# TensorE's rounds of all three stages, and attention's rounds on four engines, written out instead of looped

## The reference

```python
# tokens: normalised correlation with a 31 x 31 template, mean over 3 channels
result = conv(image, norm_template)           # same for the mean and the mean square
std    = sqrt(m2 - m1 * m1)
h      = mean_over_channels(result / (std + 1e-9)); nan -> 0      # 16 x 256 x 256

# attention: 16 query heads, 8 key heads, width 64, causal
q, k = l2norm(heads(rmsnorm(h) @ Wq)), l2norm(heads(rmsnorm(h) @ Wk));  v = ...
attn = softmax(causal(tanh(q k / 50) * 50 / 8))
h    = layernorm(h + (attn @ v) @ Wout)

# MLP, 256 -> 1024 -> 1024 -> 1024 -> 256
m = silu(x @ w1 * s1) * (x @ w2 * s2)
m = gelu(m @ h1 * t1);  m = gelu(m @ h2 * t2)
out = layernorm(h + m @ w3 * s3)
```

## Time and profile before

| | before |
|---|---|
| median of 3 runs | 1764.07 us (1761.74 to 1764.49) |
| the profiled execution | 1769.29 us |
| its span, first to last instruction | 1767.4 us |
| instructions in it | 33166 |
| TensorE busy | 1717.2 us, 97% of the span |
| VectorE busy | 1150.9 us, 65% |
| ScalarE busy | 911.1 us, 52% |
| GpSimd busy | 418.1 us, 24% |
| mean granted clock of TensorE | 0.99 of full speed |

### The profile page before, as it was taken

The page is one execution under the profiler, slowest core; times in us unless marked ns, Lnnn a source line. Parts: engine busy times, 40 slices in busy tenths (PEclk is TensorE's granted clock), DMA queues, the critical chain, the costliest instruction groups (busy, mean ns, idle before and its releaser), DMA issues. The chain is left out here.

```text
span 1767.4 us, 33166 instructions
## 1 busy us (share of the span) xinstructions
PE 1717.2 (97%) x12280; PEld 1512.0 (86%) x12280; DVE 1150.9 (65%) x2223; ACT 911.1 (52%) x1309; POOL 418.1 (24%) x517
## 2 busy tenths in 40 slices
PE   6999999999999999999999998999999999999998
PEld 5999998999987888888888887888888888888886
DVE  6999898898996878888878874342414141514242
ACT  7756555566657877886887873222222221222221
POOL 2000000000012222222222221434434333434343
PEclk9999999999999999999999998999999999999999
DMA  6222312214103002102001113500000000000000
GB/s 198 104 98 95 130 56 112 87 63 160 49 1 109 18 27 82 34 18 90 26 26 52 31 34 131 191 25 1 25 1 24 0 25 1 24 0 25 1 13 13
DMA packets 35923, 97.19 MB, mean 55 GB/s; under 512 B 3114, under 2 KB 23722, under 8 KB 31539
## 3 DMA queue, kind: packets, MB, share of 16 engines
q1 hardware_dynamic: 35762, 94.96, 15.8%
HBM read 82.33 MB, written 24.15 MB: 60 GB/s over the span
## 5 line engine op out<-in xcount | busy, mean ns | idle before, releaser
L671 PE MATMUL conv<-w,x 128*128 128x368 f16 (+5 forms) x3960 | 455.4, 279 | 1.9 <-issue 1.9
L671 PEld LDWEIGHTS conv<-w,x 128*128 128x128 f16 x3960 | 428.8, 146 | 27.1 <-issue 2.7
L1480 ACT ACTIVATE raw_c<-ring,sh 128x512 f32<-128x512 f32 x128 | 87.5, 689 | 334.4 <-PE ring L1583 334.3
L1492 DVE CAST ha_hi<-raw_c 128x512 fp32r<-128x512 f32 x128 | 83.8, 655 | 200.5 <-ACT raw_c L1480 198.3
L1439 POOL TENSOR_TENSOR ha_lo<-raw_c,ha_hi 128x512 fp32r<-128x512 f32 x128 | 165.3, 1291 | 190.9 <-DVE ha_hi L1492 190.9
L912 POOL TENSOR_SCALAR_AFFINE_SELECT probs<-probs 128x256 f32<-128x256 f32 x256 | 117.5, 482 | 362.0 <-ACT probs L981 362.0
L1583 PE MATMUL ring<-hb_lo,wh 128*128 128x512 f32 x512 | 199.5, 390 | 0.0
L1583 PE MATMUL ring<-ha_lo,wh 128*128 128x512 f32 x512 | 199.5, 390 | 0.0
L1583 PE MATMUL ring<-ha_hi,wh 128*128 128x512 f32 x512 | 199.4, 390 | 0.0
L1583 PE MATMUL ring<-hb_hi,wh 128*128 128x512 f32 x512 | 199.4, 389 | 0.0
L1179 PE MATMUL mixed<-v,probs 128*128 128x65 f32 x1536 | 188.5, 273 | 0.2 <-POOL probs L912 0.2
(11 more groups left out here) (168 smaller groups left out, 3290.2 us busy)
## 6 DMA issues: line engine op xcount, KB each, us to landing
xt<-x_columns_in SPq DMA_DIRECT2D x12, 1163.0 KB, 5.2
xp<-x_patches_in SPq DMA_DIRECT2D x12, 1152.0 KB, 5.2
hidden_words<-hidden_weights_in SPq DMA_DIRECT2D x8, 1408.0 KB, 9.1
words<-hidden_words SPq DMA_DIRECT2D x32, 352.0 KB, 3.0
wh<-hidden_words SPq DMA_DIRECT2D x8, 1024.0 KB, 10.6
tokens<-planes SPq DMA_DIRECT2D x4, 1024.0 KB, 5.6
h<-tokens SPq DMA_DIRECT2D x4, 1024.0 KB, 5.6
attended<-h SPq DMA_DIRECT2D x8, 512.0 KB, 3.4
```

The lines of the kernel that those rows point to most:

```text
L671: ins = pe.matmul(out, xs[:, c, RI - 1 - i:RI - 1 - i + NR, :, x].rearrange("p r g -> p (r g)"), w, start=(t == 0), stop=(t == size - 1), ...
L1480: act.activation(raw[:, u % 4], bank, ACT.Gelu, scale=scale[:, m:m + 1]).then_inc(s_gelu, 1)
L1492: dve.tensor_copy(dst[0][:, u % KH], raw[:, u % 4]).then_inc(s_hi, 1)
```

## The change

`planes` and `every_lot` get an argument `unrolled`, which only TensorE sets; `every_part` loses its loop for every engine that uses it. The rounds are then written one behind the other into the program by the Python that builds it, with the round number as a constant. What each round does, and in which order, stays as it is.

```diff
-        def planes(eng, body, first, start=0):
+        def planes(eng, body, first, start=0, unrolled=False):
 
 
             first()
-            with eng.Fori(start, GROUPS - 1) as g:
-                for c in range(CHANNELS):
-                    body(g, c, g * CHANNELS + c, False)
+            if unrolled:
+                for g in range(start, GROUPS - 1):
+                    for c in range(CHANNELS):
+                        body(g, c, g * CHANNELS + c, False)
+            else:
+                with eng.Fori(start, GROUPS - 1) as g:
+                    for c in range(CHANNELS):
+                        body(g, c, g * CHANNELS + c, False)
             for c in range(CHANNELS):
                 body(GROUPS - 1, c, LAST - CHANNELS + 1 + c, True)
...
-            planes(pe, body, first, 1)
+            planes(pe, body, first, 1, unrolled=True)
...
 def every_part(emit, eng):
 
-    with eng.Fori(0, GROUPS - 1) as g:
+    for g in range(GROUPS - 1):
         emit(BODY, g)
     emit(FINAL, GROUPS - 1)
...
-        def every_lot(eng, lot):
-
-            with eng.Fori(0, GROUPS - 1) as g:
-                for parity in range(2):
-                    lot(g, parity, False)
+        def every_lot(eng, lot, unrolled=False):
+
+            if unrolled:
+                for g in range(GROUPS - 1):
+                    for parity in range(2):
+                        lot(g, parity, False)
+            else:
+                with eng.Fori(0, GROUPS - 1) as g:
+                    for parity in range(2):
+                        lot(g, parity, False)
             for parity in range(2):
                 lot(GROUPS - 1, parity, parity == 1)
...
             def lots(exact):
-                every_lot(pe, lambda g, parity, last: lot(g, parity, last, exact))
+                every_lot(pe, lambda g, parity, last: lot(g, parity, last, exact), unrolled=True)
```

## The result

| | before | after |
|---|---|---|
| median | 1764.28 us, 6 runs (1761.74 to 1771.77) | 1753.11 us, 6 runs (1752.22 to 1754.22) |
| profiled execution, its span | 1769.29, 1767.4 us | 1753.59, 1751.8 us |
| mean granted clock in it | 0.990 | 0.993 |

The medians differ by 11.2 us, a ratio of 0.9937. The measured ratio with its 95% interval is 0.9924 (0.9907 to 0.9942), which is 13.4 us (10.2 to 16.4); the interval holds the 11.2 as well. The two traces differ by 15.6 us of span. Why the medians lie closer together than the traces is what experiment 1 is about.

The account below looks back on a forecast made before the run. TensorE, busy 97% of the span, was taken as the bound, so only its idle or lower-clock time counted. Seam savings of 3.75, 4.95 and 5.76 us, 14.5 in all, off 1764.07 gave 1749.6 us, range 1746.0 to 1756.5.

Parts of the forecast that it names:

- The gaps are taken branches that wait for code: At TensorE's seams between looped rounds: five idle gaps, 9.2 us, come from five taken branches waiting for code.
- The sum by seams: Saving at taken-branch seams, priced against loop exits: token stage 3.75, attention 4.95, MLP 5.76, sum 14.5 us.
- Register waits at zero: Waits on constants instead of registers gain zero; rival: 4.4 us on TensorE's path, 1745.2 us, chance 0.08.
- The other engines at zero: ScalarE, VectorE, GpSimd and SyncE, looped or written out, count zero; ScalarE's code comes 2.4 us late in attention.
- The length of the lead: TensorE's sequencer runs 1.9 us ahead of the array, hiding that much branch; queue depth would suggest 3.7 us.
- From the trace to the median: The 14.5 us priced in the 1769.29 us profiled execution, taken off the 1764.07 us median, gives 1749.6 us.
- The case called "less": Unprofiled runs lack the 5 us clock part or have cheaper branches: only 9.5 us saved, 1754.6 us, chance 0.18.
- The slower case: Straight-line fetching of written-out code fails to keep up; late packets can cost 3.5 us each; chance 0.02.

Follow-up runs that it names:

- experiment 1: The kernel before, run again with no edit: median 1764.41 us over 12 runs, ratio 0.9992.
- 4: The written-out kernel with TensorE's MLP looped again: 1753.28 us, ratio 0.9927 to the kernel before.
- experiment 5: The kernel before, all loops kept, with 111 semaphore increments at the start of TensorE's program: 1768.83 us, ratio 1.0016.
- 6: The written-out kernel with TensorE's MLP looped again and 128 semaphore increments at TensorE's start: 1766.75 us, ratio 1.0009 to the kernel before.
- experiment 7: Loops of semaphore increments added behind the kernel's work; on TensorE taken branches took 0.2 us with bodies of 32 and 1400, 3.3 to 3.5 with 1900 and 2300.
- 12: The kernel before, all loops kept, with 104 semaphore increments where TensorE waits anyway (72 at start, 20 behind token stage, 12 behind attention): 1761.68 us, ratio 0.9979.
- 2: The written-out kernel with TensorE's token stage looped again: 1756.72 us, ratio 0.9946 to the kernel before.
- experiment 3: The written-out kernel with attention looped again on all four engines: 1759.51 us, ratio 0.9959 to the kernel before.
- 9: The written-out kernel with attention looped again on TensorE alone: 1759.14 us, ratio 0.9963 to the kernel before.
- experiment 8: The written-out kernel with attention looped again on ScalarE, VectorE and GpSimd, written out on TensorE alone: 1753.93 us, ratio 0.9928 to the kernel before.
- experiment 11: The kernel before, all loops kept, with 72 semaphore increments at the start of TensorE's program: 1774.11 us, ratio 1.0042.
- 10: The written-out kernel with attention looped again on ScalarE, VectorE and GpSimd, and the MLP on TensorE: 1754.23 us, ratio 0.9928 to the kernel before.

## Why the prediction was right, and where it was off

**The gaps are taken branches that wait for code.** Right. It was argued from the times of the branches; experiments 4 to 7 and 12 show it for the MLP's loop and for bare loops, since the same branch costs 0.2 or 3.5 us by the place and size of its loop, and in the MLP instruction packets come in only where it is slow. For the token stage and attention, experiments 2, 3 and 9 show that the gaps go and come with TensorE's loop; their loops were not made to stay.

**The sum by seams.** Right to 0.1 us in the trace: 3.75, 4.95 and 5.76 us were forecast, 3.75, 4.94 and 5.75 came. Taking the exit of the loop as the measure of the seam carried that, the 0.2 us behind it included. That it agrees so closely is partly the choice of trace: the clock fell behind three gaps in that execution, and the sum took all three.

**Register waits at zero.** Right: looped and written-out planes, images and lots are equal away from the seams, and experiment 3, with the register work of the other engines in attention, is no slower than 9, without it.

**The other engines at zero.** Right for those that stay looped. For attention the prediction said that ScalarE would be late if only TensorE were written out; experiment 8 puts that at 0.5 us. The prediction gave that lateness no price, and needed none, since the change writes both out.

**The length of the lead.** The Trainium skill, "Advanced Engine Details and Errata", section "Engine Queue Depths", gives TensorE 64 entries. That these are 32 pairs worth 3.7 us was the prediction's estimate, not the page's; the trace's 1.9 us was the right number to go by. Had the queue covered the branch, kernels 2 and 3 could not have shown gaps of 2.1 and 6.0 us.

**From the trace to the median.** This is the step that was mis-sized. 14.5 us, 9.5 of idle time and 5 of clock, were taken off a median that lay 5.2 us below the profiled execution. By experiment 1 that execution, at a clock of 0.990, was among the slow ones: the 35 executions average 0.9924, the written-out kernel's six 0.9938. The difference, at 1.7 us per 0.001, makes 2.5 us of clock, not 5. With 9.5 us of idle time that is 12 us. Measured were 11.2 by the medians, and 12.4 against the 1765.5 us that the 79 later executions of the kernel before average. The other part of the miss of 3.5 us is the base itself: a median of three that lay 1.4 us below that average. Timing alone does not settle this, since the interval of the ratio, 10.2 to 16.4 us, holds 14.5 too; the clocks of the executions speak for it. The case called "less" (1754.6 us) was nearer than the forecast (1749.6), and the 5.2 us between profile and median, of just that size, were in sight. The range, 1746.0 to 1756.5, held the result.

**The slower case.** Straight code of 99 packets ran without an issue gap of over 0.2 us. Nothing speaks for it.

Open is what sets, gap by gap, whether the clock falls: in the kernel before it fell behind three of the five gaps, in its repetition behind two. Not tried, either, was a loop of the token stage or of attention small enough to stay.

## What to carry to other kernels

Read the branch instructions at a loop's line for each engine: a taken one that lasts microseconds, on the engine that sets the time, cost here its length less what the queue had in hand (3.75 us of branch, 1.94 idle), and sometimes 1.7 us of clock behind it, and the exit of the same loop, which has no taken branch, is the measure of what writing out will give. Write out the engine that is the bound first, and only loops too large to stay; the loops of the other engines in attention cost 1.2 us in all. A loop near the limit can be fast or slow by where it begins, so an edit elsewhere in that engine's program can move the time by several us in either direction. Build the forecast on several executions' clocks, not on the profiled one alone, where the clock can fall differently from run to run.

## What the runs showed of the hardware that was not expected

- TensorE kept a body of 1694 instructions for 340 us without a fetch, and one of 1400; 1900 and 2300 it fetched anew. A packet is 16 KB, about 253 instructions (25028 in 99 packets). By an estimate of where its loop begins, counted from the times at which packets came and set right once by experiment 11, the body of 1694 stayed in the four kernels in which it touches seven packets (4, 5, 10, 12) and did not in the three in which it touches eight (before, 6, 11). The Trainium skill, "Advanced Engine Details and Errata", section "ISA Cache", gives TensorE 128 KB, which fits: seven packets, 112 KB, stayed, and eight, 128 KB, did not, as if one place were taken by the packet fetched ahead. It also says lines of 16 KB and "Only 2 cache lines!", which doesn't fit: a body of seven packets could not have stayed in two.
- ScalarE kept 200 instructions and not 450; its late code cost 2.5 to 2.7 us.
- A taken branch to missing code cost TensorE 3.3 to 3.9 us; 4.1 to 4.9 in runs where, it seems, it stood just behind the start of a packet (experiments 3, 5, 9 and 12), and a gap of 4.8 and 5.1 us where its target stood some two instructions before the end of one.
- A bare semaphore increment on TensorE took 0.15 us of its program (the loops of experiment 7 as well as the late start of experiment 5), though its row shows 0.051.
